# A graph-attention and linear-attention block: the edge lists of the joint pass loaded a tile further ahead

## The reference, cut to what matters

```
x: 3125 nodes x 768; src, dst: 53125 edges, sorted by dst (self loops among them)
xn = layernorm(x)
x  = x + gnn(xn, edges) + mix(xn)      # gnn: two graph-attention layers; mix: 12 heads of kernelised attention
x  = x + ffn(layernorm(x))             # 8 experts, top 2

# first graph-attention layer, 4 heads, what the joint pass sums up
e     = leaky_relu(al_s[src] + al_d[dst], 0.2)
alpha = softmax of e over the edges of each dst
out   = segment_sum(h[src] * alpha, dst)

# the keys' half of mix
k' = exp(k @ proj - |k|^2/2 - max);  context = sum over nodes of k' v^T
```

## Time and profile before

| | |
|---|---|
| median of 3 runs | 4639.31 us (4627.12 to 4641.16) |
| the profiled execution's own time | 4635.16 us |
| its span in the trace | 4633.4 us |
| mean granted TensorE clock | 0.913 |
| TensorE busy, whole program | 3928.1 us, 85% |
| the joint pass | from 352 us (its first edge lists) to 1573 us (its last store) |

### The profile page before, as it was taken

How to read it: one execution, slowest core, us unless ns; L and a number is a source line. 1 busy time by engine, 2 the same in 40 slices (tenths; PEclk the granted TensorE clock), 3 DMA queues, 4 the chain that set the end, 5 groups by cost and what they waited for, 6 DMA issues and landing times. The chain is left out here.

```text
span 4633.4 us, 67390 instructions
## 1 busy us (share of the span) xinstructions
PE 3928.1 (85%) x23483; PEld 3147.0 (68%) x23484; DVE 2149.3 (46%) x4835; ACT 1170.5 (25%) x2391; POOL 1350.2 (29%) x1368
## 2 busy tenths in 40 slices
PE   6764988898989499996999578888878849999998
PEld 6763666666666288886999544554545449999997
DVE  6852555555555444443222144444444444444544
ACT  1231333333333233332111022222222122222222
POOL 1113655555556100000000144554555301111110
PEclk8886999999999799998999778888888969999999
DMA  5764666666676333334566466777777430000000
GB/s 207 255 247 140 222 208 216 212 216 216 215 223 215 118 139 135 140 124 127 80 80 77 151 226 220 257 250 238 259 229 241 148 117 21 27 20 20 27 20 13
DMA packets 239565, 729.54 MB, mean 157 GB/s; under 512 B 75503, under 2 KB 80650, under 8 KB 230995
## 3 DMA queue, kind: packets, MB, share of 16 engines
q0 software_dynamic: 88000, 374.95, 25.4%
q1 hardware_dynamic: 151315, 351.47, 25.0%
HBM read 642.07 MB, written 145.41 MB: 170 GB/s over the span
## 5 line engine op out<-in xcount | busy, mean ns | idle before, releaser
L873 POOL DMA_INDIRECT k_rows<-tab,k_pick x576 | 593.1, 1030 | 455.8 <-PE k_num L1293 307.7
L1996 POOL DMA_INDIRECT m_rows<-tab,m_e x500 | 486.6, 973 | 502.1 <-PE m_out L2295 313.7
L1293 PE MATMUL k_num<-k_rows,k_wt 128*64 128x385 f32 (+1 forms) x2400 | 435.8, 509 | 43.5 <-issue 38.6
L1293 PEld LDWEIGHTS k_num<-k_rows,k_wt 128*64 128x64 f32 x2400 | 171.8, 141 | 257.5 <-issue 239.7
L2275 PE MATMUL m_pj<-m_w,m_at 128*128 128x384 f32 x600 | 253.6, 582 | 28.8 <-DVE m_x L2091 22.7
L133 PE MATMUL g_prod<-g_w_hi,g_h_h 128*128 128x384 f32 x800 | 269.5, 337 | 1.5 <-DVE g_h_l L1594 1.5
L135 PE MATMUL g_prod<-g_w_hi,g_h_l 128*128 128x384 f32 x800 | 267.5, 334 | 0.0
L134 PE MATMUL g_prod<-g_w_lo,g_h_h 128*128 128x384 f32 x800 | 267.3, 334 | 0.0
L2295 PE MATMUL m_out<-m_rows,m_wt 128*32 128x384 f32 x2000 | 239.7, 513 | 22.7 <-issue 22.0
L133 PE MATMUL f_prod<-f_w_hi,f_a_h 128*128 128x512 f32 x600 | 243.9, 406 | 0.0
L2071 DVE TENSOR_REDUCE m_mx<-m_dash 128x2 f32<-128x512 f32 x150 | 103.0, 687 | 285.8 <-remote 205.5
(11 more groups left out here) (292 smaller groups left out, 8927.1 us busy)
## 6 DMA issues: line engine op xcount, KB each, us to landing
agg<-k_outb SPq DMA_DIRECT2D x100, 384.0 KB
f_a_in<-agg SPq DMA_DIRECT2D x100, 384.0 KB
h<-f_e SPq DMA_DIRECT2D x25, 1024.0 KB, 4.1
g_h<-h SPq DMA_DIRECT2D x25, 1024.0 KB, 12.9
tab<-q_xn SPq DMA_DIRECT2D x25, 388.5 KB, 6.0
tab<-g_row SPq DMA_DIRECT2D x25, 385.5 KB, 4.7
m_own<-tab SPq DMA_DIRECT2D x25, 385.5 KB
q_x<-in_x SPq DMA_DIRECT2D x25, 384.0 KB, 5.9
```

Source lines behind the costliest of these rows:

```text
L873: pool.indirect_dma_start(rows[:, place(u, n), :], None, dram["tab1"], at, bounds_check=bound, oob_is_err=False).then_inc(rows_in[i], 16)
L1293: mm = pe.matmul(num[i][64 * g:64 * g + 64, 0:n], wt[:, 2 * c + g, :], rows[:, place(u, 2 * c + g), a:a + n], start=(c == 0), stop=(c == 2 ...
L1996: pool.indirect_dma_start(rows[:, place(h, c) + k, :], None, tab, bass.IndirectOffsetOnAxis(ap=e[h % 4][:, 0, k * SLOTS + c:k * SLOTS + c ...
```

## The change

The edge lists of tile t+2 are loaded in the fourth quarter of step t, ahead of that quarter's store. Before, those of tile t+1 were loaded in the second quarter, ahead of its store. The lists of tile 1, which nothing in the loop would load now, are loaded ahead of it, behind the x tile of step 0 and ahead of the constants. The buffers and the waits inside `load_edges` stay: for tile t+2 it waits for `ef_done` of t+1, the cast of tile t's lists, which are two tiles older and have the same buffer.

```diff
--- before.py
+++ after.py
@@ -821,6 +821,8 @@
                 if merged:
                     load_edges(0)
                 load_xt(0)
+                if merged:
+                    load_edges(1)
                 sp.dma_start(pad[:, :], io["pad_rows"]).then_inc(c_in, 16)
                 if merged:
                     sp.dma_start(offs[:, :], io["group_offsets"].partition_broadcast(P)).then_inc(c_in, 16)
@@ -831,8 +833,8 @@
                             load_xt(t + 1)
                         if merged and quarter == 0 and t < NT:
                             load_ald(t)
-                        if merged and quarter == 1 and t + 1 < NT:
-                            load_edges(t + 1)
+                        if merged and quarter == 3 and t + 2 < NT:
+                            load_edges(t + 2)
                         u = set_of(t, quarter)
                         if u is not None and u >= 1:
                             store(u - 1)
```

## The result

The changed kernel took **4706.14 us** (median of four, 4693.70 to 4708.43), the one before 4639.20 beside it: ratio 1.0146 [1.0121, 1.0171], slower. The profiled execution took 4708.43 us (span 4706.4, mean granted clock 0.903 in place of 0.913). The forecast was 4695 us. But the sign doesn't hold on every chip: on a second one the same change is 0.8% *faster*, and so is its loop alone on a third. The forecast's sum for the tile with the change explains the changed kernel's part of that; the rest is that the kernel before is slower there.

The account below looks back on a forecast made before the run. The joint pass was taken as paced by SP's queue in one half of a tile and by TensorE in the other. +68 us for delayed quarters and -12 at the start, put on the median, gave 4695 us; range 4600 to 4735.

Parts of the forecast that it names:

- The new wait, its place and its chain: Joint pass: late fourth-quarter store delays the next first-quarter copy (R0); TensorE waits 4.5 us a tile at first-quarter sums.
- The 2.1 us from R0 to the sums: Joint pass: sums over edges start 2.1 us behind a late first-quarter result copy, when ScalarE's weights are ready.
- Block 21.5 us: SP's queue, fourth quarter: the edge-list DMAs hold back the store behind them by 21.5 us, mean of 22.3 and 20.7.
- the block itself grows: Rival, chance 0.08: edge-list loads in the fourth quarter take 25 us on SP's queue; +133 us, 4772 us.
- Landing 4.7: Fourth-quarter store, issued 4 us into a burst of gathers, lands in 4.7 us; lower bound 3.0, upper near 8.
- the value near 8 for a queue in order: Upper bound of the fourth-quarter store's landing, near 8 us, were it served only after the six gathers.
- Clock 2.5 us a tile: TensorE in the joint pass: its 4.5 us wait lowers the clock, 2.5 us lost in nearly every tile, period 48.8.
- Start: -12 us: Start of the joint pass: loading tile 1's lists before any gather saves 12 us, between -14 and 0.
- The sign: Whole kernel: slower, chance 0.67; faster 0.20; within 0.3% 0.13.
- the condition for a kept clock: TensorE, joint pass: a wait of 2.8 us, nearer to 2.08 than 4.02, was to cost no clock.
- The rival "faster": Chance 0.20: fourth-quarter store lands in 3.0 us, below about 3.5; TensorE waits 2.8 us, period 44.6, -36 us, 4603 us.
- The sum for the changed tile: Joint-pass period: first-quarter copy 27.3 us behind the third-quarter one, plus 2.1 and 16.9: 46.3 us; with clock loss 48.8.

Follow-up runs that it names:

- e5: The changed kernel run again without an edit, on chip C: 4470.05 us, ratio 0.9917 to the kernel before.

## Why the prediction was right on A, and would have been wrong on B and C

- **The new wait, its place and its chain: right.** R3's store late behind the block, R0 late behind the store, TensorE at the first-quarter sums, and nothing left at the transposes. The 2.1 us from R0 to the sums was 1.9 (1067.31 to 1069.21), and TensorE's wait 5.1 us in the mean, where 4.5 was forecast.
- **Block 21.5 us: too short on A**, 23.4 (24.6 on D); it stretches beside the gathers on those chips, where on B and C it is 20.9. The rival "the block itself grows" was right in kind, not in size.
- **Landing 4.7: near**, 4.3 in the mean, 3.1 to 6.2. By the Trainium skill (DMA: Bandwidth & Descriptors, Queues, rings and completion order) queues share a DMA engine by the packet; a store 4.2 us into a burst that lands in 4.8 agrees with it, and the value near 8 for a queue in order did not come.
- **Clock 2.5 us a tile: too high.** The leg R0 to R2 took 20.3 us in the mean, where 2.1 + 16.9 + 2.5 = 21.5 was forecast: 1.3 us over the sum without the clock, not 2.5. This made up for the block, which is luck: 48.8 forecast, 48.6 measured.
- **"Start: -12 us": the step that failed.** The first part came true: load_edges(1) ended at 393.9, and the second transposes came at 399.25, 15 us sooner. But then the 21 gathers ran beside the first logits, VectorE and ScalarE stood still until 431.0 ("remote", not explained), and SP took up to 7.7 us between two issues. The first copy came 1.3 us later than before, just outside the bound 0 of the two that I gave, and on C, where the trace has no such standstill, it came 4.7 us later, with a wait of 5.0 us for the rows; the start alone measured 1.0005 there. The term left out what the gathers, moved along with their lists, cost the first logits. It also put the 35 us of load_edges(1) down to the 21 gathers beside it, and on C, beside the same gathers, that load is as short as any other (2.3 us a group).
- **The sign: the condition for a kept clock was wrong, and the kernel before was taken as fixed.** The rival "faster" decides at a landing of 3.5 with a block of 21.5, a sum of 25.0, because a wait of 2.8 us was to cost no clock. On B and C the sum is 24.9 and 24.8, and TensorE's wait is 2.8 us in the mean on C. But the clock falls in 21 of 22 tiles there all the same, and the period is 45.7, not that rival's 44.6. Against the 45.7 of the kernel before on A this would be level. It is a gain on C because the kernel before takes 47.7 there: its own store lands in 4.6 us, and it loses clock in every tile. (B has no trace of the kernel before.) On A and D the sum is 27.7 and 29.1, and the change loses.
- **The sum for the changed tile held.** 1.1 + block + landing + 2.1 + 16.9, without the clock, gives 47.8, 45.0, 44.9 and 49.2 us for A to D; measured are 0.4 to 1.0 us more. The forecast took block and landing from one trace as if they were the kernel's, and they are the chip's too.

Not settled: what the "remote" waits are, and why A and D have them and B and C none. They appear in the two phases with gathers (tiles k_ and m_), in both kernels, and in no other. The Trainium skill (Runtime: NRT & Kernel Launch, Instruction fetch mechanics) says that each engine's sequencer fetches its instructions through a DMA queue of its own; no run here shows that this is what waits.

## What to carry to other kernels

A load that is early enough can still set the pace by standing in a queue ahead of something urgent. Before moving it, count what its issue takes and look at what stands behind it in the new place; splitting it, or a second buffer for what stands behind it, gave 3% on B (splitting 1% on D), where moving it gave 0.8% or cost 1.5 to 1.9%. Where a change trades one wait of 2 to 5 us on TensorE for another, the sign can differ between chips, so repeat both kernels on a second one before keeping it.

## What the runs showed of the hardware

- Two small DMAs whose address comes from a register loaded just before them took 2.3 us on SP's queue of chips B and C, 2.5 on A and 2.7 on D, means over the tiles of the changed loop; with constant addresses 1.1 on D (899.58 to 907.17, seven groups). One more load, whose value nothing used, cost only 0.5 us. Whether the rest is the wait for the value or the making of the addresses wasn't separated.
- The same 384 KB store lands in 2.6 to 6.7 us beside gathers. In the kernel before it took 2.6 to 3.6 us when issued at most 0.45 us into a burst, and 4.1 to 5.1 when issued 0.55 to 1.25 us into one.
- A wait of TensorE of 2.02 us was followed by a granted clock of 0.58 (e5), one of 2.08 by 1.00. The length of the wait alone doesn't tell which of the two comes.
- The same kernel takes 4505 us on two chips and 4640 on two others. Most of this lies outside the change: behind R0 of tile 24 the changed kernel took 3156 us on A and 3003 on C (4471.7 - 1469.19). On A the waits named "remote" in that part come to 317 us on VectorE and 395 on ScalarE (tiles m_), on C to none.
